# Turning a transpose into the place where candidate cells are folded: one product each on GpSimd, more matmuls on TensorE

## The chip, the cores and the metric

One core of a Trainium2 chip runs the whole program. The metric is the device time in microseconds of one execution, the median of several. Engines: PE is TensorE, DVE is VectorE, ACT is ScalarE, POOL is GpSimd, SP is SyncE, which issues the DMAs.

## What is computed

```python
frames = x.reshape(32, 313, 128)             # padded audio
h = einsum('bfh,kh->bfk', frames, D)         # DCT
h = h + attention(layernorm(h))              # within each of the 32 clips
# peer expert layer on layernorm(h), 8 heads:
s0, s1 = ...                                 # scores against 64 + 64 keys
sc0, ix0 = top_k(s0, 16); sc1, ix1 = top_k(s1, 16)
cs = sc0[..., :, None] + sc1[..., None, :]   # 16 x 16 sums per head
ci = ix0[..., :, None] + ix1[..., None, :]
fs, pos = top_k(cs, 16); fi = ci[pos]; w = softmax(fs)
inner = hidden . expert_down[fi]; act = gelu(inner)
h = h + sum((act * w) * expert_up[fi])
```

Of the 256 sums of a head only those at (i, j) with (i + 1)(j + 1) <= 16 can be among the 16 largest. The kernel forms 54 cells that hold these, in five rectangles (`CAND`, line 28). Since an index is a sum of two numbers below 64, only 128 expert rows are ever addressed.

## The kernel before

The 32 clips are taken in 16 pairs (`k`). A pair has 626 rows, in five tiles of 128 rows (`t` = 0 to 4), 80 tiles in all. The program of every engine is written out by hand in the same order (`drive`, line 266): for each tile four parts `p` = 0 to 3, in each of which `slot(k, t, p)` issues expert work and `front(k + 1, t, p)` the dense work of the next pair (DCT, attention, projection, statistics). Engines meet by semaphores. A tile's expert work is spread over five tiles' time, so that in one slot different engines work on different tiles.

What a tile goes through, with its lines:

- DVE takes the 16 largest of 64 scores for 16 half heads (p 1 and 2: `MAX8` L1016 and L1023, `MATCH_REPLACE8` L1019, `FIND_INDEX8` L1025 and L1028).
- POOL forms the sums of scores, `cs`, and of indices, `ci`, with one add per rectangle (`cells`, L822 to L830; `cs` in p 0, `ci` in p 1 after a wait for the `beta` of DVE).
- DVE takes the 16 largest of the 54 cells per head in p 3: `MAX8` over the first `NC8` = 44 cells (L1076), `MATCH_REPLACE8` (L1079), `MAX8` over 54 (L1082), `MATCH_REPLACE8` (L1085). The first 44 cells hold every cell that can be among the 8 largest. `c2` then has the value `PICKED` at the chosen cells.
- ACT makes the mask `m` from `c2` (L670) and the exponentials (L672). POOL multiplies by the reciprocal sum (`wz`, L869), then makes `Yw` = weights x mask and `Ye` = indices x mask (L873 to L877): one product over cells 0 to 31 and, for each, six small ones over the other 22 cells, which are put on 32 places of a second block (`share`, L833). Then it signals `y_full`. In p 3 it makes `bw` (L884, three products of 1024 elements), which waits for `w3_full` and `beta_full`.
- PE transposes and adds in p 3 (`rows`, L484, called at L532 to L536): for each half `a` of four heads it multiplies both blocks by the identity into the same 128 columns of PSUM, so that two cells which can't both be chosen share a row. `Ye` (bf16) goes to `STE`, `Yw` (f32) to `U`. A float32 matmul shows as two instructions in the trace.
- DVE reads `STE` in p 1 of the next tile: `hi` (L1035, L1040), `lo` (L1042), then eight comparisons of 1024 bf16 elements into `alpha` (L1049) and four into `beta` (L1055). This stretch is called the alpha phase below.
- ACT and PE split the weights in `U` into three bf16 parts (L677, L705, L708 on ACT, `less` L495 on PE), PE multiplies `alpha` and `bw` (L528, 16 matmuls in each part p, the first of a tile waits for `bw_full`).

Dense work that lies around it: at (2,1) DVE forms a seed (L953, L902), POOL runs 12 small Newton steps (L752), ACT makes `hid` (L639), PE transposes it at (2,2) (L394) and multiplies by `WcT` at (2,2) and (3,0) (L437). PE's statistics, called VAR below (L446, L447), come at (3,2). DVE reads them at (3,3) in `front`, behind its p 3 work (L978), and PE's `rows` for slot (2,3) lies in this chain. At (3,3) POOL starts another Newton chain when DVE has read VAR. `inner` (L459 to L470) has matmuls whose weights have 32 columns, with results at 32, 64 and 96 of the partitions.

Of the kernel before, what the change touches and what calls it, by code (L numbers as in the profile page):

```python
# [8 lines left out]
BF16 = mybir.dt.bfloat16  # L9
I32 = mybir.dt.int32  # L10
U32 = mybir.dt.uint32
ALU = mybir.AluOpType
# [14 lines left out]

CAND = [(0, 1, 16, 0), (1, 1, 8, 16), (2, 2, 5, 24), (4, 4, 3, 34), (8, 8, 1, 46)]
NC = 54
NC8 = 44  # L30
NX, NY = 32, 4
NS = 4
NG, NQ = 4, 32
# [44 lines left out]
def build(nc, x, Wq, bq, ln_g, ln_b, keys0, keys1, down, up, ident_d, dct_d, indc_d, sel_d, row8_d, sel3_d, out):  # L78
# [4 lines left out]
    with ctx:  # L83
# [93 lines left out]
        m = sb("m", [128, H, NC])  # L177
        wexp = sb("wexp", [128, H, NC])
        wz = sb("wz", [128, H, NC])
        Yw = sb("Yw", [128, 2, H, 32])  # L180
        Ye = sb("Ye", [128, 2, H, 32], BF16)
        wp = sb("wp", [128, 3, 3, 256], BF16)
        hi = sb("hi", [128, NS, 256], BF16)
        lo = sb("lo", [128, 256], BF16)
# [184 lines left out]
        def _(pe):  # L369
# [114 lines left out]
            def rows(src, eye, dst, end):  # L484

                for a in range(2):
                    for blk in range(2):
                        cells = src[:, blk, 4 * a:4 * a + 4, :].rearrange("p h r -> p (h r)")
                        last = mm(dst[:, 128 * a:128 * a + 128], cells, eye[:], start=(a == 0 and blk == 0),  # L489
                                  stop=(end and a == 1 and blk == 1), skip_group_check=True)  # L490
                return last

            def less(buf, i):
# [248 lines left out]
        def _(pool):  # L742
# [12 lines left out]
            def setup():  # L755
                nc.gpsimd.memset(xin[:], 0.0)
                nc.gpsimd.memset(ss[0][:], 1.0)
                nc.gpsimd.memset(ss[1][:], 1.0)
                nc.gpsimd.memset(c15[:], 1.5)
                nc.gpsimd.memset(one[:], 1.0)  # L760
                nc.gpsimd.memset(kp[:], 0.0).then_inc(s["zeroed"], 1)
                nc.gpsimd.memset(xns[:], 1.0)
                nc.gpsimd.memset(stdin[:], 0.0)
                nc.gpsimd.memset(Gd[:], 0.0)
                nc.gpsimd.memset(Yw[:], 0.0)
                nc.gpsimd.memset(Ye[:], 0.0)
                nc.gpsimd.memset(cneg64[:], -SHIFT)
                nc.gpsimd.memset(cpick[:], PICKED + 1.0)
                nc.gpsimd.memset(cquart[:], -0.75).then_inc(s["zeroed"], 1)
                pool.wait_ge(s["zeroed"], 2)  # L770
                nc.gpsimd.memset(stdin[:, :, 0, :, 8:9], 1.0)
                pool.wait_ge(s["kseed_full"], 1)
                newton(ky[:], kxh[:], ka[:], c15[0:64, 0:2], s["knewton"], 0)
# [48 lines left out]
            def cells(dst, v, done):  # L822

                halves = v.rearrange("p (h a) r -> p h a r", a=2)
                for i0, ni, nj, off in CAND:
                    o = dst[:, :, off:off + ni * nj].rearrange("p h (i j) -> p h i j", i=ni)
                    a0 = halves[:, :, 0, i0:i0 + ni].unsqueeze(3).to_broadcast([128, H, ni, nj])
                    a1 = halves[:, :, 1, 0:nj].unsqueeze(2).to_broadcast([128, H, ni, nj])
                    last = tt(o, a0, a1, ALU.add)  # L829
                last.then_inc(done, 1)  # L830


            share = [(slice(34, 44, 3), slice(12, 16)), (slice(35, 45, 3), slice(8, 12)),  # L833
                     (slice(46, 50), slice(20, 24)), (slice(50, 54), slice(4, 8)),
                     (slice(32, 33), slice(28, 29)), (slice(36, 37), slice(27, 28))]

            def slot(k, t, p):
                n = NT * k + t
# [26 lines left out]
                if p == 2 and exists(k, t, 2):  # L865
# [5 lines left out]
                    pool.wait_ge(s["m_full"], n - 1)  # L871
                    after(pool, s["st_full"], n - 2)
                    for Y, src in ((Yw, wz[:]), (Ye, ci[:, buf, :, :])):  # L873
                        tt(Y[:, 0, :, :], src[:, :, 0:32], m[:, :, 0:32], ALU.mult)
                        for cell, row in share:
                            last = tt(Y[:, 1, :, row], src[:, :, cell], m[:, :, cell], ALU.mult)
                    last.then_inc(s["y_full"], 1)  # L877
                if p == 3 and exists(k, t, 3):
                    buf = RING[(t - 3) % NT]
# [298 lines left out]
```

## Time and profile before

| | |
|---|---|
| median of 3 runs | 2131.66 us (2131.37 to 2132.61) |
| the profiled execution | 2132.51 us, its span 2130.3 us |
| mean granted PE clock | 0.729 of 2.4 GHz |
| DVE | busy 2008.6 us (94%), 16198 instructions |
| PE | 1682.7 us (79%) |
| POOL | 1578.8 us (74%) |
| ACT | 1108.1 us (52%) |
| DMA | 10 GB/s over the span |
| chain that ended last | DVE 68%, PE 14%, POOL 8%, issue 6%, ACT 3% |

The shares of the chain tell on which engine's work the end depended, step by step, and DVE's idle time tells where something else was late. A pair takes some 125 us, a tile some 25 us.

### The profile page before, as it was taken

The page shows a single profiled execution, that of the slowest core. Times are in us where ns is not written, and L with a number is a line of the kernel's source. Part 1 is how long each engine was busy: PE and PEld are TensorE (multiplying, and loading weights), DVE is VectorE, ACT ScalarE, POOL GpSimd, SP SyncE. Part 2 cuts the span into 40 slices and gives each one's busy share as a digit, 9 for nine tenths or more (in the row PEclk, how much of TensorE's full clock was granted, in tenths as well). Part 3 has the DMA queues.
Part 4 walks back from the last instruction along what each step waited for, and adds up shares of the span by engine and source line. Part 5 has one row for each costly group of instructions (what it writes and reads, how often), then busy time and mean ns, then how long its engine had stood idle before and what let it go on. Part 6 is the DMA issues. An engine that isn't in the chain of part 4 may idle for free.

```text
span 2130.3 us, 48144 instructions
## 1 busy us (share of the span) xinstructions
PE 1682.7 (79%) x10975; PEld 1311.4 (62%) x10975; DVE 2008.6 (94%) x16198; ACT 1108.1 (52%) x3515; POOL 1578.8 (74%) x3519
## 2 busy tenths in 40 slices
PE   5567698877869887797888779788877988887666
PEld 3336576655747665575766657666665756666455
DVE  3299999999999999999999999999999999999993
ACT  3344555565555556555555555545555564554443
POOL 2237788787778878777887877788787877878775
PEclk9676877677776777768677686867767686776655
DMA  1000000000000000000000000000000000000000
GB/s 34 13 9 2 18 7 13 14 6 18 6 18 6 8 18 8 18 6 19 7 6 18 9 18 6 18 6 6 19 9 16 9 18 6 6 12 9 6 8 9
DMA packets 46676, 24.86 MB, mean 12 GB/s; under 512 B 4955, under 2 KB 46116, under 8 KB 46390
## 3 DMA queue, kind: packets, MB, share of 16 engines
q1 hardware_dynamic: 46390, 21.80, 3.7%
q8 instruction: 88, 1.44, 0.3%
q14 instruction: 198, 1.62, 0.3%
HBM read 11.52 MB, written 10.26 MB: 10 GB/s over the span
## 4 chain that ended last, share of the span: by engine, by line
DVE 68%; PE 14%; POOL 8%; issue 6%; ACT 3%; another core or an unknown queue 0%; SPq 0%; DMA 0%; DVEq 0%; POOLq 0%; ACTq 0%
DVE hrest L1019 10%; DVE alpha L1049 8%; DVE idx L1025 8%; DVE idx L1028 8%; DVE vals L1016 6%; DVE vals L1023 5%; DVE crest L1079 4%; DVE c L1085 4%; PE FB L446 3%; PE FB L437 3%; PE QB L528 3%; DVE top L1082 2%; POOL bw L884 2%; DVE top L1076 2%; DVE beta L1055 2%
## 5 line engine op out<-in xcount | busy, mean ns | idle before, releaser
L528 PE MATMUL QB<-bw,alpha 128*128 128x48 bf16 x5120 | 553.3, 277 | 62.7 <-issue 62.0
L528 PEld LDWEIGHTS QB<-bw,alpha 128*128 128x128 bf16 x5120 | 521.5, 151 | 101.9 <-issue 93.0
L884 POOL TENSOR_TENSOR bw<-beta,wp 128x1024 bf16<-128x1024 bf16 x240 | 503.9, 2129 | 10.3 <-ACT wp L708 9.9
L722 ACT ACTIVATE WD<-QB 32x96 f32<-32x96 f32 x1280 | 307.2, 240 | 91.9 <-PE QB L528 80.4
L1049 DVE TENSOR_SCALAR alpha<-hi 128x1024 bf16<-128x1024 bf16 x640 | 270.0, 493 | 0.0
L480 PE MATMUL SC<-WK,hidT 128*128 128x512 f32 x320 | 225.3, 794 | 38.8 <-ACT hidT L655 23.9
L829 POOL TENSOR_TENSOR ci<-idxf 128x64 f32<-128x64 f32 (+3 forms) x400 | 123.9, 343 | 177.2 <-DVE beta L1055 176.9
L1025 DVE FIND_INDEX8 idx<-vals,sraw 128x8 uint32<-128x64 f32 x1280 | 250.5, 218 | 0.0
L1028 DVE FIND_INDEX8 idx<-vals,hrest 128x8 uint32<-128x64 f32 x1280 | 250.5, 219 | 0.0
L1019 DVE MATCH_REPLACE8 hrest<-vals,sraw 128x64 f32<-128x64 f32 x1280 | 250.2, 209 | 0.0
L1016 DVE MAX8 vals<-sraw 128x8 f32<-128x64 f32 x1280 | 169.2, 209 | 0.0
L1023 DVE MAX8 vals<-hrest 128x8 f32<-128x64 f32 x1280 | 167.3, 208 | 0.0
L752 POOL TENSOR_TENSOR sa<-sy 128x6 f32<-128x6 f32 x96 | 19.7, 205 | 193.0 <-DVE sy L902 188.0
L715 ACT ACTIVATE ofin<-QB 128x128 f32<-128x128 f32 x80 | 22.2, 277 | 263.9 <-PE QB L528 261.0
L829 POOL TENSOR_TENSOR cs<-vs 128x64 f32<-128x64 f32 (+3 forms) x400 | 137.0, 375 | 6.3
L437 PE MATMUL FB<-hidTn,WcT 128*128 128x313 f32 x256 | 121.3, 633 | 19.9 <-ACT hidTn L645 10.8
L480 PEld LDWEIGHTS SC<-WK,hidT 128*128 128x128 f32 x320 | 72.4, 246 | 97.7 <-issue 53.4
L446 PE MATMUL FB<-indc,sq 128*128 128x24 f32 x640 | 127.4, 347 | 0.7 <-ACT sq L650 0.7
L516 PE MATMUL QB<-upR,Gd 128*128 128x128 f32 x640 | 123.7, 355 | 4.5 <-issue 4.2
L702 ACT ACTIVATE sraw<-SC 128x1024 f32<-128x1024 f32 x80 | 83.1, 1038 | 83.1 <-PE SC L481 82.4
L446 PEld LDWEIGHTS FB<-indc,sq 128*128 128x128 f32 x640 | 122.9, 285 | 1.1 <-ACT sq L650 1.1
L489 PE MATMUL U<-ident,Yw 128*128 128x128 f32 x640 | 121.1, 350 | 0.0
(206 smaller groups left out, 4079.9 us busy)
## 6 DMA issues: line engine op xcount, KB each, us to landing
res<-h_scratch SPq DMA_DIRECT2D x80, 64.0 KB, 1.8
xin<-in_x SPq DMA_DIRECT2D x32, 128.0 KB
h_scratch<-h2n SPq DMA_DIRECT2D x32, 128.0 KB
out<-ofin SPq DMA_DIRECT2D x64, 64.0 KB, 1.6
h_scratch<-h2n SPq DMA_DIRECT2D x32, 28.5 KB
out<-ofin SPq DMA_DIRECT2D x16, 57.0 KB
xin<-in_x SPq DMA_DIRECT2D x32, 28.0 KB
xin<-in_x SPq DMA_DIRECT2D x32, 0.2 KB
```

The source lines that it names most:

```text
L446: mm(bank[:, 40 * tt:40 * tt + 24], sq[:, c, cols], indc[:, c, :], start=(c == 0), stop=(c == 3))
L480: mm(SC[:, cols], hidT[:, START[t1]:START[t1] + 128], WK[:, cols], start=True, stop=False)
L528: last = mm(bank[:, 48 * u:48 * u + 48], alpha[:, buf, a, :, 8 * p + u], bwv[:, :, a, :, 8 * p + u], start=(a == 0), stop=(a == 1))
L722: last = A(WD[r, RING[(t - 4) % NT], :, 8 * p:8 * p + 8], blocks[r, :, :, g], ACT.Copy)
L829: last = tt(o, a0, a1, ALU.add)
L884: last = tt(bw[:, buf, NY * i:NY * i + NY, :], beta[:, buf, :, :], wp[:, buf, i, :].unsqueeze(1).to_broadcast([128, NY, 256]), ALU.mult)
L1016: V.max(vals[:, buf, i, 0:8], raw[i]).then_inc(chain, 1)
L1019: V.match_replace(rest[i], vals[:, buf, i, 0:8], raw[i], -1e30).then_inc(chain, 1)
L1023: V.max(vals[:, buf, i, 8:16], rest[i]).then_inc(chain, 1)
L1025: V.max_index(idx[:, buf, i, 0:8], vals[:, buf, i, 0:8], raw[i]).then_inc(chain, 1)
L1028: last = V.max_index(idx[:, buf, i, 8:16], vals[:, buf, i, 8:16], rest[i])
L1049: last = V.tensor_scalar(a8[:, :, :, xx, :], h8, float(NY * xx), None, ALU.is_equal)
```

## The change

`Yw` and `Ye` are stored cell by cell ([54 cells, 8 heads] in each partition), so POOL makes each with one product over all 54 cells and 8 heads, writing with a step of 8 elements. The sharing of rows moves to PE: `rows` multiplies cells 0 to 15 and 16 to 31 as before (a = 0, 1), and then six more groups of 16 or 32 columns each (`FOLD`), written on top of partitions 32, 64 or 96 of the same PSUM columns. Rectangle (4,4,3), cells 34 to 45, is stored with i innermost, so that each fold is a run of cells and the first 38 cells hold all that can be among the 8 largest: `NC8` goes from 44 to 38. Two memsets of the setup go.

```diff
-NC8 = 44
+NC8 = 38
+FOLD = [(slice(34, 38), 0, 12), (slice(38, 42), 0, 8), (slice(42, 46), 0, 4), (slice(50, 54), 0, 4),
+        (slice(46, 50), 1, 4), (slice(32, 34), 1, 12)]
...
-        Yw = sb("Yw", [128, 2, H, 32])
-        Ye = sb("Ye", [128, 2, H, 32], BF16)
+        Yw = sb("Yw", [128, NC, H])
+        Ye = sb("Ye", [128, NC, H], BF16)
...
                 for a in range(2):
-                    for blk in range(2):
-                        cells = src[:, blk, 4 * a:4 * a + 4, :].rearrange("p h r -> p (h r)")
-                        last = mm(dst[:, 128 * a:128 * a + 128], cells, eye[:], start=(a == 0 and blk == 0),
-                                  stop=(end and a == 1 and blk == 1), skip_group_check=True)
+                    last = mm(dst[:, 128 * a:128 * a + 128], src[:, 16 * a:16 * a + 16, :].rearrange("p c h -> p (c h)"),
+                              eye[:], start=(a == 0), stop=False, skip_group_check=True)
+                for i, (cells, a, row) in enumerate(FOLD):
+                    w = H * (cells.stop - cells.start)
+                    last = mm(dst[8 * row:8 * row + w, 128 * a:128 * a + 128],
+                              src[:, cells, :].rearrange("p c h -> p (c h)"), eye[:], start=False,
+                              stop=(end and i == len(FOLD) - 1), skip_group_check=True)
...
-                nc.gpsimd.memset(Yw[:], 0.0)
-                nc.gpsimd.memset(Ye[:], 0.0)
...
-                    o = dst[:, :, off:off + ni * nj].rearrange("p h (i j) -> p h i j", i=ni)
+                    by = "p h (j i) -> p h i j" if i0 == 4 else "p h (i j) -> p h i j"
+                    o = dst[:, :, off:off + ni * nj].rearrange(by, i=ni)
...
-            share = [(slice(34, 44, 3), slice(12, 16)), (slice(35, 45, 3), slice(8, 12)),
-                     (slice(46, 50), slice(20, 24)), (slice(50, 54), slice(4, 8)),
-                     (slice(32, 33), slice(28, 29)), (slice(36, 37), slice(27, 28))]
...
                     for Y, src in ((Yw, wz[:]), (Ye, ci[:, buf, :, :])):
-                        tt(Y[:, 0, :, :], src[:, :, 0:32], m[:, :, 0:32], ALU.mult)
-                        for cell, row in share:
-                            last = tt(Y[:, 1, :, row], src[:, :, cell], m[:, :, cell], ALU.mult)
+                        last = tt(Y[:].rearrange("p c h -> p h c"), src, m[:], ALU.mult)
```

## Rows read from the trace of the kernel before

**Rows 1.** The page: busy time, share of the span and instructions of each engine
```profile
PE 1682.7 (79%) x10975; PEld 1311.4 (62%) x10975; DVE 2008.6 (94%) x16198; ACT 1108.1 (52%) x3515; POOL 1578.8 (74%) x3519
```

**Rows 2.** Waits of DVE: line, releaser, us in total, times, longest
```profile
DVE v L978 <- PE FB L447: 27.7, 10, 22.7
```

**Rows 3.** Timeline, two pairs' ends of VAR: start us, us, engine, line, [idle before]
```profile
1046.35 0.20 DVE L978 TENSOR_SCALAR v<-FB 128x40 f32<-128x40 f32 x1 [0.49 <-PE FB L447]
...
1168.56 0.59 PE L447 MATMUL FB<-WB,hidTn 128*128 128x16 f32 x2
...
1170.98 0.20 DVE L978 TENSOR_SCALAR v<-FB 128x40 f32<-128x40 f32 x1
```

**Rows 4.** Groups by line and form, DVE's MAX8: count, busy us, mean ns
```profile
L1082 DVE MAX8 top<-crest 128x8 f32<-128x54 f32 x640 | 81.4, 200 | 0.0
...
L1076 DVE MAX8 top<-cs 128x8 f32<-128x44 f32 x640 | 74.8, 190 | 0.0
```

**Rows 5.** Timeline of POOL, from the first product of one tile
```profile
1015.14 0.73 POOL L874 TENSOR_TENSOR Yw<-wz,m 128x256 f32<-128x256 f32 x1
...
1017.78 1.33 POOL L876 TENSOR_TENSOR Ye<-ci,m 128x32 bf16<-128x32 f32 x6
1019.04 6.32 POOL L884 TENSOR_TENSOR bw<-beta,wp 128x1024 bf16<-128x1024 bf16 x3
...
1027.54 1.55 POOL L829 TENSOR_TENSOR cs<-vs 128x128 f32<-128x128 f32 x5
```

**Rows 6.** Groups by line and form, POOL's longer products
```profile
L884 POOL TENSOR_TENSOR bw<-beta,wp 128x1024 bf16<-128x1024 bf16 x240 | 503.9, 2129 | 10.3 <-ACT wp L708 9.9
...
L869 POOL TENSOR_TENSOR wz<-wexp,rz 128x432 f32<-128x432 f32 x80 | 72.7, 909 | 3.7 <-DVE rz L1067 3.7
```

**Rows 7.** Groups at 1016.1 us, and at 1016.6 us, of POOL
```profile
L876 POOL TENSOR_TENSOR Yw<-wz,m 128x32 f32<-128x32 f32 x2 | 0.5, 286 | 0.0
...
L876 POOL TENSOR_TENSOR Yw<-wz,m 128x32 f32<-128x32 f32 x1 | 0.3, 265 | 0.0
```

**Rows 8.** Busy us (instructions) in four alpha phases: PE, PEld, DVE, ACT, POOL, PEclk
```profile
1027.54:1032.50 4.96, 4.96 (x13) 2.55 (x12) 4.92 (x19) 3.78 (x11) 1.54 (x5) 0.74 0.00 2
1052.12:1059.08 6.96, 4.58 (x88) 4.20 (x87) 6.92 (x19) 6.10 (x16) 6.33 (x15) 0.75 0.03 8
1077.61:1082.11 4.50, 1.98 (x18) 1.64 (x17) 4.47 (x19) 4.38 (x14) 0.00 (x0) 0.91 0.02 5
1102.16:1108.77 6.61, 6.61 (x26) 3.24 (x25) 6.58 (x19) 4.97 (x14) 5.63 (x13) 0.77 0.01 2
```

**Rows 9.** Timeline of PE around `rows` in the chain to VAR
```profile
1022.99 0.40 PE L489 MATMUL EB<-identb,Ye 128*128 128x128 bf16 x4
1023.23 1.11 PE L489 MATMUL U<-ident,Yw 128*128 128x128 f32 x8
1025.46 1.74 PE L528 MATMUL QB<-bw,alpha 128*128 128x48 bf16 x16 [1.11 <-issue]
```

**Rows 10.** Timeline of PE: `rows`, then the start and the end of `inner`
```profile
1172.82 0.61 PE L489 MATMUL EB<-identb,Ye 128*128 128x128 bf16 x4
...
1175.17 0.68 PE L467 MATMUL SC<-hidT,DT 128*32 128x128 f32 x8
...
1177.33 0.89 PE L528 MATMUL QB<-bw,alpha 128*128 128x48 bf16 x7
```

**Rows 11.** Busy us in these two calls of `rows`, columns as in rows 8
```profile
1022.99:1024.34 1.35, 1.35 (x15) 1.16 (x12) 1.35 (x12) 1.10 (x5) 1.35 (x2) 1.00 0.00 0
1172.82:1175.17 2.35, 2.35 (x14) 2.13 (x13) 2.35 (x24) 2.08 (x8) 1.80 (x7) 0.50 0.18 52
```

**Rows 12.** Timeline of POOL and DVE in the last tiles
```profile
2076.88 6.27 POOL L884 TENSOR_TENSOR bw<-beta,wp 128x1024 bf16<-128x1024 bf16 x3
...
2077.97 6.23 DVE L1040 TENSOR_SCALAR hi<-hi 128x256 bf16<-128x256 bf16 x3
...
2093.31 6.26 POOL L884 TENSOR_TENSOR bw<-beta,wp 128x1024 bf16<-128x1024 bf16 x3
```

## The prediction

> **What bounds the kernel now.** I read the page's busy times first: DVE is busy 94% of the span, PE 79%, POOL 74% [rows 1]. Then the waits of DVE, to see where it isn't the bound. In the middle of the run it waits in one place only, for VAR: 10 times, 27.7 us, of which the first, in the fill, is 22.7, so nine waits of 0.55 us on average, 5.0 us together [rows 2]. The timeline at this place shows two kinds of pairs. In nine pairs DVE comes 0.4 to 0.7 us too early (at 1046 us it idles 0.49); in five others it comes 1.9 us after VAR was done (VAR's last matmul ends at 1169.15, DVE's L978 follows its own work at 1170.98), and in an early one 5.8 us after [rows 3]. So two chains of nearly equal length run from DVE's seed at (2,1) to L978 at (3,3): DVE's own work, and POOL's Newton steps, `hid`, PE's projection, `rows`, the quads and VAR. Everywhere else DVE alone sets the pace. What makes DVE faster counts in full outside this stretch, and inside it only as far as PE's chain gets faster too.
>
> Last I asked whether DVE's work always takes as long. The table of alpha phases says no: the same 19 instructions take 4.50 us while POOL is idle, 4.96 with 1.54 us of POOL's work inside, 6.61 with 5.63 and 6.96 with 6.33 [rows 8]. Each us of POOL's work in an alpha phase costs DVE 0.30 us (0.46 / 1.54) to 0.39 (2.46 / 6.33). POOL is thus on the path, though it is idle a quarter of the time. Where it comes before, its adds must end before DVE's alpha phase starts.
>
> **The change part by part.**
>
> (a) **MAX8 over 38 cells in place of 44.** 54 cells take 200 ns, 44 take 190, 1 ns per cell [rows 4]. 6 cells x 1.0 ns x 640 = 3.8 us of DVE.
>
> (b) **POOL's products.** Now `Yw` starts at 1015.14 and `bw` at 1019.04: 3.90 us for 14 instructions [rows 5]. After, there are two of 432 elements. A product that reads two full tensors takes 0.73 us for 256 elements [rows 5], and 2.129 us for 1024 [rows 6]: 1.82 ns per element, so 0.73 + 176 x 0.00182 = 1.05 us for 432. `wz` with its 432 took 0.909, but one operand is repeated [rows 6]. That is the lower end. The write has a step of 8 elements, which no POOL instruction of the trace has. The nearest row is a read with a step of 3: 286 ns against 265 for 32 elements [rows 7], 0.6 ns per element for two stepped reads. I take the same for the one stepped write: 1.05 + 432 x 0.0006 = 1.3 us. Two take 2.6, and POOL is s = 1.3 us earlier with `bw`. Bounds: s = 1.8 with no penalty; s = 0 if a product takes 1.95 us, nearly twice the unstepped one. Below nothing is possible, since nothing in the trace excludes a penalty over twofold.
>
> GPSIMD Engine Reference of the Trainium skill, section Performance pitfalls for Q7 kernels, says that reads whose step is over 8 bytes cost half as much again. The trace shows 8% for a step of 12 bytes [rows 7]; the page says nothing of writes. Applied to these writes it is a rival below.
>
> (c) **What s does to alpha phases.** Two of five tiles gain. At (3,1) (14 pairs show it) `cs` starts at 1027.54 and lasts 1.55, inside the alpha phase [rows 5, 8]; 1.3 us earlier nearly all of it lies before the phase: 0.46 x 14 = 6.4 us. At (1,1) POOL goes without a pause from its products through `bw`, a Newton chain and its adds into the phase; 1.3 us less overlap at (6.61 - 4.50) / 5.63 = 0.37 is 0.48, x 15 = 7.2 us. At (4,1) the POOL chain is started by DVE's L978, so it isn't earlier: nothing. The other two have no overlap: nothing.
>
> (d) **PE's folds and the chain to VAR.** `rows` now takes 1.35 us at a granted clock of 1.00 (2.4 GHz) and 2.35 at 0.50 (1.2 GHz), for four products of each kind [rows 11]. After, there are two full ones and six narrow ones of each kind. `inner` shows what narrow ones cost: 16 float32 products of 128 columns and 16 of 32, to all four column groups, take from 1175.17 to 1177.33, 2.16 us [rows 10], at 0.50. One after the other they would take about 10 us (2.0 us for four full ones [rows 10, 11], so 0.5 and 0.125 each). So four groups run side by side. The six folds go to groups 3, 2, 1, 1, 1, 3: three places in a row, with the two full ones five in place of four. I take + 1.35 / 4 = 0.34 us; the upper end, nothing side by side, is + 1.35. In the chain to VAR PE now stands still for 1.11 us behind `rows` [rows 9], until POOL's `bw` ends at 1025.36 [rows 5]. After, `rows` ends at 1024.34 + 0.34 = 1024.68, and `bw` at 1025.36 - 1.3 = 1024.06. PE goes on 0.78 us earlier than at 1025.46.
>
> DVE's own part of the stretch gets 0.46 (c) + 0.10 (MAX8 of two tiles) = 0.56 us shorter. Where DVE waits now, the pair gains what PE gains, 0.78, which is 0.22 more than (a) and (c) count: x 9 = 2.0 us. In the pairs with 1.9 us of slack nothing is added. In the other tiles the folds lie on PE's idle time: DVE needs only the `Ye` part of `rows`, first in order, and waits for it nowhere in the middle.
>
> TensorEngine Tiling (Array Packing) of the Trainium skill, section Tiling Modes, says that a change of tiling mode drains TensorE, and the change brings four per tile. The trace shows none between `rows` and `inner`: `inner` starts at 1175.17, when `rows` ends [rows 10, 11]. The page gives no price, so the sum stays.
>
> (e) **The last tiles.** There the `bw` of POOL (2076.88 to 2083.15) holds up a DVE instruction that else takes 0.2 us (L1040, three in 6.23 us), and PE's quads too [rows 12]. Two sets of products lie on this path, ahead of the `bw` at 2076.88 and at 2093.31 [rows 12]: 2 x 1.3 = 2.6, and some 0.4 of overlap goes in the alpha phase before: 3.0 us. The two memsets of the setup lie beside loads: nothing. The turned rectangle changes the step of one write of `cs` and `ci` each; at 96 elements x 0.6 ns it is 0.06 us ahead of `bw`, nothing to count.
>
> Sum: 3.8 + 6.4 + 7.2 + 2.0 + 3.0 = 22.4 us. The profiled execution took 2132.51, its span 2130.3; the median of the runs is 0.85 below the profiled one, and I take the gain from the median: 2131.7 - 22.4 = 2109.3 us, in a profile about 2110.
>
> **The rivals.**
>
> *All waits for VAR go.* PE's clock is 0.50 or 1.00 by stretches [rows 11], and a PE that no longer stands still may keep 1.00 in the projection behind. With s at 1.8 too: 3.8 + 6.4 + 15 x 0.67 + 5.0 + 4.0 = 29.2, so 2102.5. For it: the slack pairs have exactly this. Against: VAR itself runs at 0.50 for most of its time in both kinds.
>
> *Folds don't overlap.* Then `rows` ends at 1025.69 and PE is 0.23 later than now, and what DVE gains in the stretch is lost too: -9 x (0.23 + 0.56) = -7.1 in place of +2.0. 22.4 - 9.1 = 13.3: 2118.4. Against it stands `inner`; for it, that three folds in a row go to one group, and that the others are few.
>
> *Stepped writes cost half as much again* (the rule on reads named above, taken for writes). 1.58 us per product, s = 0.74: (a) 3.8; (c) 0.22 x 14 + 0.27 x 15 = 7.1; (d) PE still gains 0.78 against 0.32 of DVE, 9 x 0.46 = 4.1; (e) 1.7. Sum 16.7: 2115.0.
>
> *Stepped writes cost double, POOL isn't earlier.* s = 0: 3.8 from MAX8, less 0.9 that DVE now waits for VAR: 2.9, so 2128.8. The change then has nothing but its shorter MAX8.
>
> *Slower: PE's chain becomes the bound.* If the folds run one by one and narrow columns leave the clock at 0.50 at (2,3) in every pair, `rows` takes 4.7 us there and ends at 1027.69, 2.23 us later than PE goes on now. Nine pairs lose 9 x 2.23 = 20.1, the five with slack 0.9 each, together 24.6; what is gained outside the stretch, 2.3 + 7.2 + 3.0 = 12.5, stays. 2131.7 + 12 = 2144. It decides from about 1.4 us per waiting pair (12.5 / 9). For it: the clock is low in these very matmuls in other places [rows 11]. Against: at (2,3) they stand at 1.00 after a long busy stretch.
>
> **How the numbers follow.** Forecast 0.42, all waits gone 0.13, folds in a row 0.15, half as much again 0.12, double 0.10, slower 0.08. The predicted time is that of the forecast, 2109. About 0.2% (4.3 us) can be told from no change: faster 0.82, same 0.10, slower 0.08. The range leaves out the last two, 0.18, and reaches from 2101 (s = 1.8 and all waits gone, with 1.5 us for what the clock may add) to 2126 (folds in a row together with half as much again, some 2123, and a few us for the clock).
>
> **What would show it.** MAX8 of L1076 at 184 ns. Two POOL products of 1.3 us each and `bw` 1.3 us after where it would be without; 1.05 or 1.95 tell the ends. The alpha phase at (3,1) at 4.5 us and at (1,1) at 6.1; at (4,1) as before. Behind `rows` at (2,3) no gap of PE; `rows` itself 1.7 us at clock 1.00 (forecast) or 2.7 (in a row). The wait of DVE for VAR, 0.55 us in nine pairs, at 0.3. The prediction is wrong if POOL's products aren't shorter, if alpha phases don't follow POOL's overlap, or if waits for VAR grow in pairs that had none.

## The result and the profile after

The changed kernel takes 2116.74 us (2116.2 to 2117.8, 4 runs) against 2132.14 of the kernel before in the same runs: a ratio of 0.9926, 95% interval 0.9909 to 0.9944, so 15.4 us faster, 12 to 19. The forecast was 22.4 us, 2109.3; the measured time lies inside its range of 2101 to 2126. Its profiled execution took 2116.96 us with a span of 2115.2 and a mean granted clock of 0.744.

Busy times on the page of the changed kernel (as rows 1):

```profile
PE 1727.9 (82%) x11935; PEld 1335.8 (63%) x11935; DVE 1993.5 (94%) x16198; ACT 1108.9 (52%) x3515; POOL 1501.2 (71%) x2557
```

DVE has 15.1 us less work with the same 16198 instructions, and the span is 15.1 us shorter. Since MAX8 explains 3.9 us of this (below), the larger part is DVE's time for instructions that the diff doesn't touch. PE has 45 us more work, POOL 78 us less.

The groups by line and form, changed kernel, with POOL's products and MAX8 (as rows 4 and 6): count, busy us, mean ns.

```profile
L874 POOL TENSOR_TENSOR Ye<-ci,m 128x432 bf16<-128x432 f32 x80 | 173.3, 2167 | 0.0
...
L874 POOL TENSOR_TENSOR Yw<-wz,m 128x432 f32<-128x432 f32 x80 | 89.0, 1113 | 6.3
...
L1074 DVE MAX8 top<-cs 128x8 f32<-128x38 f32 x640 | 70.9, 185 | 0.0
```

The two products differ in the type that they write (and in which tensor they read beside the mask), and the record of the bf16 one is twice as long. The timeline of POOL in the same tile as rows 5, changed kernel:

```profile
1007.13 1.10 POOL L874 TENSOR_TENSOR Yw<-wz,m 128x432 f32<-128x432 f32 x1
1008.19 2.12 POOL L874 TENSOR_TENSOR Ye<-ci,m 128x432 bf16<-128x432 f32 x1
1009.91 6.38 POOL L882 TENSOR_TENSOR bw<-beta,wp 128x1024 bf16<-128x1024 bf16 x3
1017.66 0.46 POOL L842 TENSOR_TENSOR ws<-WD 128x128 f32<-128x128 f32 x1 [1.38 <-ACT WD L727]
```

From the first product to `bw` it is 2.78 us in place of 3.90 [rows 5]: POOL is 1.12 us earlier. From start to start the float32 product holds POOL up for 1.06 us and the bf16 one for 1.72, since `bw` starts before `Ye` is recorded as ended. But then POOL stands still for 1.38 us ahead of `ws`, for ACT's `WD`: part of what was won is lost here.

The timeline of PE at the same place (as rows 9), changed kernel:

```profile
1016.21 0.29 PE L489 MATMUL EB<-identb,Ye 128*128 128x128 bf16 x2
1016.43 0.35 PE L493 MATMUL EB<-identb,Ye 128*32 128x128 bf16 x6
1016.71 0.71 PE L489 MATMUL U<-ident,Yw 128*128 128x128 f32 x4
1017.35 0.86 PE L493 MATMUL U<-ident,Yw 128*32 128x128 f32 x12
1018.14 1.77 PE L533 MATMUL QB<-bw,alpha 128*128 128x48 bf16 x16
```

`rows` takes 1.93 us until the next matmul starts (1016.21 to 1018.14). To the end of its last record it is 2.00, against the 1.35 of before [rows 9, 11], which is taken that way. The gap of PE behind it is gone. Six float32 folds take 0.79 us, two and a half times a full product (0.64 / 2 = 0.32). The six bf16 folds take 0.28, and a full bf16 product 0.11.

The waits of DVE and of POOL in the changed kernel (as rows 2): in total us, times, longest.

```profile
DVE v L976 <- PE FB L449: 28.6, 7, 22.0
...
POOL ci L833 <- DVE beta L1053: 136.1, 40, 11.7
POOL ci L833 <- ACT idxf L694: 59.0, 11, 5.9
...
POOL ws L842 <- ACT WD L727: 17.6, 8, 9.1
```

Without the first one, DVE waits 6.6 us for VAR in six pairs (1.1 each), before 5.0 in nine. POOL waits 59 us for ACT's `idxf`, where it waited 0.3 before. Most of that is time in which it would have waited for `beta` in any case: both waits together are 195 us, before 177. POOL's wait for ACT's `wp` ahead of `bw` grows too, from 9.9 us to 36.2, but not in the tiles that lead to the alpha phases at (3,1) and (1,1). The pairs now alternate: a quick one (123.9 us) in which VAR comes 1.2 to 1.4 us before it is needed, and a slow one (125.3 us) in which it comes 1.1 us late. Before they took 124.7, 125.5 and 125.3 us in turn.

The stages of a slow pair's chain to VAR (from PE's transposes of `hid` through the projection; `rows` to the quads; VAR) in the changed kernel, columns as in rows 8; the first and the last of these stages in a quick pair; and four alpha phases: (3,1) of a slow and a quick pair, (1,1) of a pair behind a slow one and of one behind a quick one.

```profile
1005.85:1016.21 10.36, 9.59 (x40) 6.97 (x41) 10.36 (x105) 4.81 (x14) 10.28 (x8) 0.59 0.01 2
1016.20:1028.20 12.00, 11.44 (x91) 8.68 (x89) 11.93 (x83) 9.99 (x29) 7.39 (x17) 0.99 0.05 13
1028.20:1038.85 10.65, 10.65 (x54) 10.65 (x51) 9.69 (x100) 0.97 (x4) 8.09 (x5) 0.50 0.00 0
...
1131.52:1140.54 9.02, 8.24 (x41) 5.86 (x42) 9.02 (x94) 4.81 (x14) 8.94 (x8) 0.68 0.01 3
1152.53:1161.65 9.12, 9.12 (x53) 9.12 (x52) 9.12 (x95) 0.97 (x4) 8.85 (x5) 0.60 0.00 1
...
1019.41:1024.53 5.12, 4.56 (x19) 2.57 (x18) 5.09 (x19) 4.35 (x13) 2.21 (x6) 1.00 0.01 2
1145.09:1149.65 4.56, 4.00 (x16) 2.18 (x16) 4.53 (x19) 3.54 (x10) 0.64 (x3) 1.00 0.01 2
1094.30:1101.26 6.96, 5.84 (x32) 3.42 (x31) 6.93 (x19) 5.58 (x16) 6.30 (x14) 1.00 0.00 0
1218.57:1224.85 6.28, 5.62 (x20) 2.73 (x21) 6.25 (x19) 3.52 (x9) 4.80 (x11) 0.73 0.01 1
```

The alpha phase follows POOL's share as before [rows 8], but only every other pair has the relief: at (3,1) 4.56 us with 0.64 us of POOL, or 5.12 with 2.21; at (1,1) 6.28 with 4.80, or 6.96 with 6.30. (The 19 instructions of such a row are the 17 of the phase and two that touch its ends.) In a slow pair VAR runs at 0.50 (1.2 GHz) from beginning to end, in a quick one at 0.60 on average.

What makes POOL late for the alpha phase at (1,1) begins at (4,3). First `rows` there in the kernel before, at 2.4 GHz, then in the changed kernel behind a slow pair's VAR, with what PE, ACT and POOL do next:

```profile
1192.35 0.40 PE L489 MATMUL EB<-identb,Ye 128*128 128x128 bf16 x4
1193.53 1.15 PE L394 MATMUL FB<-ident,xin 128*128 128x128 f32 x6
```

```profile
1064.39 0.39 PE L489 MATMUL EB<-identb,Ye 128*128 128x128 bf16 x2
...
1066.30 1.50 PE L493 MATMUL U<-ident,Yw 128*32 128x128 f32 x12
1067.73 1.50 PE L396 MATMUL FB<-ident,xin 128*128 128x128 f32 x5
...
1068.75 0.43 ACT L603 ACTIVATE xT<-FB 128x313 f32<-128x313 f32 x1 [2.98 <-PE FB L396]
...
1075.77 0.50 ACT L694 ACTIVATE idxf<-idx,cquart 128x256 f32<-128x256 uint32 x1
...
1076.42 1.55 POOL L833 TENSOR_TENSOR ci<-idxf 128x128 f32<-128x128 f32 x5 [5.85 <-ACT idxf L694]
```

Before, `rows` at (4,3) kept PE for 1.2 us at 2.4 GHz or 2.2 at 1.2 GHz. Now it runs at 1.2 GHz in most pairs, quick and slow, and takes 3.3 us. Where it does so behind a quick pair's VAR, it starts 7.1 us before DVE's alpha phase at (0,1), and `idxf` starts 4.4 us into that phase, whose `beta` ends at 4.5: POOL's `ci` is 0.5 us late. Behind a slow pair's VAR PE is 1.2 us later, `idxf` starts 5.5 us into the phase, and `ci` is 1.6 us late.

### The profile page after: what moved, and what is told of

It is laid out like the page before. It is cut to its first block, busy times and chain, and to the rows that moved or that the text cites. A ratio compares the mean times of both kernels' runs of the same rounds, so it can differ in the third digit from the quotient of the medians.

```text
span 2115.2 us, 49102 instructions
## 1 busy us (share of the span) xinstructions
PE 1727.9 (82%) x11935; PEld 1335.8 (63%) x11935; DVE 1993.5 (94%) x16198; ACT 1108.9 (52%) x3515; POOL 1501.2 (71%) x2557
## 4 chain that ended last, share of the span: by engine, by line
DVE 78%; PE 12%; issue 4%; ACT 2%; POOL 2%; another core or an unknown queue 0%; SPq 0%; DMA 0%; DVEq 0%; POOLq 0%; ACTq 0%
DVE hrest L1017 11%; DVE idx L1023 10%; DVE idx L1026 10%; DVE alpha L1047 9%; DVE vals L1014 7%; DVE vals L1021 6%; DVE crest L1077 5%; DVE c L1083 5%; DVE top L1080 3%; PE FB L448 3%; DVE top L1074 2%; DVE beta L1053 2%; PE QB L533 2%; PE FB L439 2%; DVE hi L1038 2%
## 5 line engine op out<-in xcount | busy, mean ns | idle before, releaser
L882 POOL TENSOR_TENSOR bw<-beta,wp 128x1024 bf16<-128x1024 bf16 x240 | 508.1, 2146 | 36.5 <-ACT wp L713 36.2
L1047 DVE TENSOR_SCALAR alpha<-hi 128x1024 bf16<-128x1024 bf16 x640 | 265.6, 488 | 0.0
L482 PE MATMUL SC<-WK,hidT 128*128 128x512 f32 x320 | 211.0, 747 | 35.4 <-ACT hidT L660 33.4
L874 POOL TENSOR_TENSOR Ye<-ci,m 128x432 bf16<-128x432 f32 x80 | 173.3, 2167 | 0.0
L521 PE MATMUL QB<-upR,Gd 128*128 128x128 f32 x640 | 136.3, 382 | 4.5 <-issue 4.2
L448 PE MATMUL FB<-indc,sq 128*128 128x24 f32 x640 | 134.3, 359 | 0.7 <-ACT sq L655 0.7
L448 PEld LDWEIGHTS FB<-indc,sq 128*128 128x128 f32 x640 | 129.8, 299 | 1.1 <-ACT sq L655 1.1
L521 PEld LDWEIGHTS QB<-upR,Gd 128*128 128x128 f32 x640 | 124.6, 286 | 8.4 <-issue 6.8
L500 PE MATMUL U<-wp,minusb 128*128 128x256 bf16 x160 | 52.7, 329 | 92.6 <-ACT wp L710 81.3
L439 PE MATMUL FB<-hidTn,WcT 128*128 128x313 f32 x256 | 109.3, 577 | 20.0 <-ACT hidTn L650 10.9
## 6 DMA issues: line engine op xcount, KB each, us to landing
h_scratch<-h2n SPq DMA_DIRECT2D x32, 28.5 KB
```

The lines of the kernel that those rows point to most:

```text
L448: mm(bank[:, 40 * tt:40 * tt + 24], sq[:, c, cols], indc[:, c, :], start=(c == 0), stop=(c == 3))
L521: mm(FO, Gd[:, y, :], upR[:, y, :], start=(y == 0), stop=False)
L882: last = tt(bw[:, buf, NY * i:NY * i + NY, :], beta[:, buf, :, :], wp[:, buf, i, :].unsqueeze(1).to_broadcast([128, NY, 256]), ALU.mult)
L1047: last = V.tensor_scalar(a8[:, :, :, xx, :], h8, float(NY * xx), None, ALU.is_equal)
```

## The experiments

All times are medians; "before" is the kernel before in the same runs, 2130.6 to 2132.3 us, and ratios are to it. The changed kernel was timed only for the result above (ratio 0.9926). Since "before" itself lies up to 1.8 us apart, a difference to 2116.74 of 2 us or less isn't shown by the times alone. A profile is of one execution, up to 3.4 us from the median. The sums over alpha phases below are over the first 15 pairs, as the excess over 4.50 us each: in the kernel before 7.1 us at (3,1) and 30.2 at (1,1), in the changed one 4.5 and 28.5.

**MAX8 alone.**

```diff
-NC8 = 44
+NC8 = 38
...
+                    by = "p h (j i) -> p h i j" if i0 == 4 else "p h (i j) -> p h i j"
...
-            share = [(slice(34, 44, 3), slice(12, 16)), (slice(35, 45, 3), slice(8, 12)),
+            share = [(slice(34, 38), slice(12, 16)), (slice(38, 42), slice(8, 12)),
...
-                     (slice(32, 33), slice(28, 29)), (slice(36, 37), slice(27, 28))]
+                     (slice(32, 33), slice(28, 29)), (slice(42, 43), slice(27, 28))]
```

> The kernel before with nothing changed but the turned rectangle and MAX8 over 38 cells (the products of POOL and the transposes of PE stay). If time goes by DVE's work and the waits for VAR: 3.9 us less work of DVE, of which 0.1 us per waiting pair is lost in longer waits, so about 3 us faster (2129). If instead the clock of PE follows each small shift of the program, the pattern of pairs changes and the time may move by several us either way (2124 to 2136).

2129.32 us, ratio 0.9986 (0.9977 to 0.9996): 2.8 us faster, 0.9 to 4.9. DVE's MAX8 has 3.9 us less, and its waits for VAR rise from 27.7 to 30.5 us in the profile (of an execution of 2131.4 us). The pattern of pairs did change, too: 13 pairs wait in place of nine. So this part of the change is worth about 3 us, as expected here; the interval holds the 3.8 of the prediction as well. What it frees is partly taken back at VAR.

**POOL as late as before.**

```diff
-                    for Y, src in ((Yw, wz[:]), (Ye, ci[:, buf, :, :])):
+                    for Y, src in ((Yx, wz[:]), (Yw, wz[:]), (Ye, ci[:, buf, :, :])):
```

`Yx` is a new tile of the shape and type of `Yw`.

> The changed kernel with one more product on POOL (the weights a second time, into a tile that nobody reads), so that POOL is as late with bw as before the change, and folds and MAX8 stay. If POOL's earlier bw brought what isn't MAX8, this gives it back: some 2.2 us in the last tiles and 4 to 6 us in the alpha phases, 2123 to 2126, with alpha phases at (3,1) and (1,1) as long as before. If POOL isn't what counts, it stays within 2 us of the changed kernel (2117).

2128.48 us (2125.06 to 2129.26), ratio 0.9982 (0.9973 to 0.9992). One product of 1.1 us that nobody reads, as long as the lead that the changed kernel has won, costs 11.7 of the 15.4 us. (1,1) has an excess of 32.5 us, more than before the change, and (3,1) 6.2. The median is above the range that I expected, in the direction of the first theory. The profile is of a faster execution (2126.49). In it 9.5 us are lost: 4.3 between the first VAR and the last, 3.3 in the last tiles, and 1.9 before the first VAR, a start that varies between kernels (below). The first two, 7.6 us, are what the profiles put down to POOL's lead. So POOL's lead ahead of `bw` carries at least half of the gain, and by the medians nearly all that isn't MAX8, though POOL is idle 29% of the time.

**No folds.** The cells 32 to 53 are left out of the result.

```diff
-                for i, (cells, a, row) in enumerate(FOLD):
+                for i, (cells, a, row) in enumerate([]):
```

The second full product of `Yw` then closes the sum in PSUM (`stop`), as the last fold did.

> The changed kernel without the six folds in either transpose: cells 32 to 53 are left out of the result. rows then takes 0.9 us at 2.4 GHz and 1.5 at 1.2, against 1.9 and 3.3. If the folds' time on PE took the missing part of the gain (later VAR, and in pairs at 1.2 GHz a later ACT and so a later POOL), the waits for VAR fall from 6.6 us to under 2 and the alpha phase at (1,1) is 6.2 us in all pairs: 2107 to 2110. If the missing part lies with POOL's slow product of indices, it stays at 2115 to 2117.

2111.53 us (2110.02 to 2112.8), ratio 0.9905 (0.9889 to 0.9922): the folds cost 5.2 us. The waits in this kernel:

```profile
POOL ci L833 <- DVE beta L1053: 210.5, 50, 11.8
DVE v L976 <- PE FB L449: 24.3, 5, 21.5
...
POOL ci L833 <- ACT idxf L694: 0.3, 1, 0.3
```

POOL no longer waits for `idxf`, and (1,1) has an excess of 23.4 us with the relief in every pair. The waits for VAR are 2.8 us, and there is still a slow pair in three. The time misses the expected 2107 to 2110 by 1.5 us and the waits for VAR the expected 2 by 0.8; the places were those expected. `idxf` now starts at most 2.4 us into the alpha phase at (0,1), well ahead of `beta`. So the chain is PE's `rows` at (4,3), then the dense work behind it, then ACT, in whose queue `idxf` stands behind that work, then POOL. The edit takes the folds out of all five tiles, so that it is (4,3) rests on the times above and on the next experiment.

**`idxf` ahead of the dense work.** PE is untouched.

```diff
-                if p == 0 and exists(k, t, 1):
-                    buf = RING[(t - 1) % NT]
-                    act.wait_ge(s["halves_full"], n)
-                    after(act, s["ci_full"], n - 1)
-                    A(idxf[:], idx[:, buf, :, :], ACT.Identity, bias=cquart[:]).then_inc(s["idxf_full"], 1)
...
+                if p == 3 and exists(k, t, 0):
+                    act.wait_ge(s["halves_full"], n + 1)
+                    after(act, s["ci_full"], n)
+                    A(idxf[:], idx[:, RING[t], :, :], ACT.Identity, bias=cquart[:]).then_inc(s["idxf_full"], 1)
```

> The changed kernel with ACT's conversion of the indices moved from p 0 of the next tile to the end of p 3, ahead of the dense work of the front. Nothing changes on PE. If the alpha phases at (1,1) stay long in the slow pairs because POOL waits for ACT's idxf (59 us in the changed kernel), these waits go, that phase is 6.2 us in every pair, and the time is 3 to 5 us less (2112 to 2114), with VAR chains and their waits as in the changed kernel. If POOL was late for another reason, the time stays at 2116 to 2117, or rises where ACT now waits for DVE's halves.

2115.20 us (2115.01 to 2115.51), ratio 0.9927 (0.991 to 0.9943). That is 1.5 us under the changed kernel's 2116.74, but "before" is 1.6 us lower here too, and the ratios are the same: the times show no gain, where I had expected 3 to 5 us. The profiles show one of 2.4 us between the first VAR and the last. The mechanism is right: no wait of POOL for `idxf` any more, the excess at (1,1) falls from 28.5 to 24.0 us, 6.1 to 6.3 us in every pair. Little of it reached the time, and DVE's rows tell why. The longest of DVE's norms at (0,1), first the changed kernel, then this one:

```profile
L991 DVE SCALAR_TENSOR_TENSOR n<-v,n 128x80 f32<-128x80 f32 x16 | 4.7, 296 | 0.5
```

```profile
L990 DVE SCALAR_TENSOR_TENSOR n<-v,n 128x80 f32<-128x80 f32 x16 | 6.4, 398 | 0.5
```

POOL's `ci`, no longer late, now runs right behind `beta`, beside these steps of DVE: from the end of the alpha phase to the next candidate stage it takes 10.1 us, where it took 9.7 in the pairs in which POOL was late. Of 0.7 us won at (1,1) 0.4 is given back at (0,1). Over 15 pairs the norms give back 2.8 us of 4.5.

**The product of indices with a packed write**, alone and with the early `idxf`:

```diff
-                        last = tt(Y[:].rearrange("p c h -> p h c"), src, m[:], ALU.mult)
+                        if Y is Ye:
+                            last = tt(Y[:], src.rearrange("p h c -> p c h"), m[:].rearrange("p h c -> p c h"), ALU.mult)
+                        else:
+                            last = tt(Y[:].rearrange("p c h -> p h c"), src, m[:], ALU.mult)
```

> The changed kernel with the product of indices taken cell by cell: its two reads have a step of 54 elements (216 bytes) and its write in bf16 is packed. If only the stepped bf16 write is dear (2.12 us against 1.06 for the float32 one), the product takes 1.1 to 1.6 us and the kernel gains 1 to 4 us (2113 to 2116). If stepped reads are as dear, it takes 2 us or more and nothing is gained (2117 or later).

2116.47 us (2116.34 to 2116.83), ratio 0.9928 (0.9912 to 0.9945). The product takes 1751 ns in place of 2167, but `bw` starts 1.62 us behind its start where it was 1.72, and nothing clear is gained: by what POOL's queue pays, the stepped reads cost about what the stepped write did.

> The same move together with the product of indices taken cell by cell (packed bf16 write, stepped reads). If POOL's work ahead of bw counts by itself, this adds 0.5 to 1.5 us to the gain of the move alone (2111 to 2113). If not, it equals it.

2113.35 us (2113.04 to 2115.34), ratio 0.992 (0.9904 to 0.9937), 1.9 us below the early `idxf` alone in the same runs (one of its four times lies inside the other's range), with an excess of 22.9 us at (1,1). The excess at (1,1) explains 1.1 us of it.

**Another order of the folds.**

```diff
-FOLD = [(slice(34, 38), 0, 12), (slice(38, 42), 0, 8), (slice(42, 46), 0, 4), (slice(50, 54), 0, 4),
-        (slice(46, 50), 1, 4), (slice(32, 34), 1, 12)]
+FOLD = [(slice(42, 46), 0, 4), (slice(34, 38), 0, 12), (slice(38, 42), 0, 8), (slice(50, 54), 0, 4),
+        (slice(32, 34), 1, 12), (slice(46, 50), 1, 4)]
```

> The changed kernel with the six folds in another order, by column group 1, 3, 2, 1, 3, 1 in place of 3, 2, 1, 1, 1, 3, so that no more than one follows another in the same group. If same-group folds wait for each other, the six float32 folds take about 0.7 us in place of 0.79 at 2.4 GHz, the pairs keep their pattern and the time is within 2 us of the changed kernel. If the price is that of issuing 18 instructions, the folds take the same time, and so does the kernel (2116 to 2118).

2119.05 us (2117.95 to 2120.07). The float32 folds take 0.77 us in place of 0.79, `rows` 1.91: the order is worth nothing. The time is 2.3 us above the changed kernel, and outside what I expected. That is not from the pairs, whose pattern is the same: DVE reads the first VAR at 75.5 us in this profile and at 73.2 in that of the changed kernel, and in the other kernels shown here between 72.8 and 75.1. What sets this start was not tried.

**`cs` ahead of `ws`.** POOL's five adds for `cs` come before the three that need ACT's `WD`.

```diff
-                if p == 0 and exists(k, t, 5):
-                    pool.wait_ge(s["wd_full"], 4 * (n - 4))
...
                     cells(cs[:, buf, :, :], vs[:], s["cs_full"])
+                if p == 0 and exists(k, t, 5):
+                    pool.wait_ge(s["wd_full"], 4 * (n - 4))
```

> The changed kernel with POOL's sums of scores (vs, cs) ahead of its adds of PE's results (ws, G) in p 0. If the alpha phase at (3,1) kept its length because POOL stands behind ACT's WD (1.4 us at 1016 us) with cs behind it, cs now lies before that phase: its excess falls from 4.5 us to under 2. The time falls only by what isn't taken back at VAR: in the slow pairs DVE waits longer for it, so 0 to 3 us (2114 to 2117). If POOL was late for another reason, the excess stays at 4 or more.

2114.76 us (2111.36 to 2115.36), ratio 0.9917 (0.9901 to 0.9934). Its alpha phases at (3,1) and (1,1), columns as in rows 8:

```profile
1017.04:1021.53 4.49, 3.94 (x17) 2.40 (x16) 4.46 (x19) 3.72 (x12) 0.50 (x2) 1.00 0.00 2
1091.84:1098.53 6.69, 5.57 (x29) 3.14 (x29) 6.66 (x19) 2.98 (x10) 6.01 (x14) 1.00 0.00 0
```

At (3,1) the excess is 0.0 us in all 15 pairs, from 4.5. So what stood ahead of `cs` in POOL's queue kept it late. The edit takes `cs` past the wait for `WD` and past three adds of 1.5 us as well. That the wait was the cause is worked out from the profile of the changed kernel: the six pairs without relief are those in which POOL waited 1.3 to 1.4 us for `WD`. Without it `cs`, which starts at 1019.87 in the pair shown, would end some 0.6 us inside the phase, as it does in the quick pairs. In the four slow pairs that are left the wait for VAR grows from 1.1 to 1.8 us, so that nothing is gained in them; two pairs that were slow are now quick. This profile is of the fastest execution, 3.4 us under the median, and the median doesn't differ clearly from the changed kernel's.

**POOL's writes by themselves.** Two programs with POOL alone, 432 elements per product, 8 of each; most of the result is left out.

The first program writes float32 at steps of 4, 8 and 32 bytes (f1, f2, f8) and bf16 at 2, 4, 8 and 16 bytes (h1, h2, h4, h8), and has two forms with packed writes whose reads are both at a step of 216 bytes (fr, hr). The second writes only bf16: packed (plain), at 4, 8 and 16 bytes with the values between them written by the same instruction (twomix, fourmix, eightmix), and at 16 and 32 bytes with each value alone (eight, sixteen).

> Nothing of the computation: POOL alone makes products of 432 elements, 8 times each, into tiles with different steps and types (the result is left out but for 128 rows of ones). If a step of over 8 bytes in a write costs half as much again whatever the type, f8 (float32, step 32 bytes), h8 (bf16, 16 bytes) and h4 take 1.6 us against 1.06 for f1 and h1. If the trouble is that a stepped bf16 write touches part of a word, h2, h4 and h8 all take 2.1 us, and f2 and f8 1.06. Stepped reads of 216 bytes (fr, hr) take 1.6 to 1.75.

Groups of single products in the first program (f1; h4; h8), and the two with stepped reads:

```profile
L60 POOL TENSOR_TENSOR f<-a,b 128x432 f32<-128x432 f32 x1 | 1.1, 1093 | 0.1
...
L60 POOL TENSOR_TENSOR h<-a,b 128x432 bf16<-128x432 f32 x1 | 1.2, 1157 | 0.0
...
L60 POOL TENSOR_TENSOR h<-a,b 128x432 bf16<-128x432 f32 x1 | 2.1, 2111 | 0.0
...
L60 POOL TENSOR_TENSOR fr<-a,b 128x432 f32<-128x432 f32 x8 | 13.1, 1641 | 0.0
L60 POOL TENSOR_TENSOR hr<-a,b 128x432 bf16<-128x432 f32 x8 | 13.0, 1630 | 0.0
```

All three float32 forms take 1.09 to 1.10 us, bf16 at 2, 4 and 8 bytes 1.09, 1.10 and 1.16, and only bf16 at 16 bytes 2.11. Neither theory said this. From its start to the start of the next product, which is what the queue pays, the last one takes 1.71 us and the other six forms 1.05.

> POOL alone again, 432 elements each, all written in bf16: packed; eight values interleaved at a step of 16 bytes (as in the change); the same step with each value alone in its 16 bytes; alone in 32 bytes; four interleaved at 8 bytes; two at 4 bytes. The result is left out but for 128 rows of ones. If the step of 16 bytes is what costs, the first lone one takes 2.1 us and that of 32 bytes as much or more, and those of 8 and 4 bytes 1.1. If interleaving is what costs (a value next to one written shortly before), the lone ones take 1.1 us and all interleaved ones 2.1.

```profile
L57 POOL TENSOR_TENSOR eight<-a,b 128x432 bf16<-128x432 f32 x8 | 18.5, 2313 | 0.0
L57 POOL TENSOR_TENSOR sixteen<-a,b 128x432 bf16<-128x432 f32 x8 | 17.7, 2212 | 0.0
L57 POOL TENSOR_TENSOR eightmix<-a,b 128x432 bf16<-128x432 f32 x8 | 16.9, 2107 | 0.0
L57 POOL TENSOR_TENSOR fourmix<-a,b 128x432 bf16<-128x432 f32 x8 | 10.7, 1335 | 0.0
L57 POOL TENSOR_TENSOR twomix<-a,b 128x432 bf16<-128x432 f32 x8 | 8.9, 1109 | 0.0
L57 POOL TENSOR_TENSOR plain<-a,b 128x432 bf16<-128x432 f32 x8 | 8.7, 1092 | 0.6
```

A value alone in its 16 or 32 bytes is as slow as an interleaved one (from start to start 1.91 and 1.84 us, against 1.71), so for bf16 it is the step and not the interleaving. Why float32 at 32 bytes is free stays open. GPSIMD Engine Reference of the Trainium skill (Performance pitfalls for Q7 kernels) has half as much again for reads over 8 bytes. The reads at 216 bytes agree (1.64 against 1.09 us). The writes, of which the page says nothing, don't follow that rule: float32 pays nothing, and bf16 at 16 bytes pays more.

**Everything stored cell by cell from the start**, on top of the early `idxf`:

```diff
-        ci = sb("ci", [128, 3, H, NC])
+        ci = sb("ci", [128, 3, NC, H])
...
-                    A(m[:], c2[:], ACT.Relu, scale=-1.0, bias=cpick[:]).then_inc(s["m_full"], 1)
+                    A(m[:].rearrange("p c h -> p h c"), c2[:], ACT.Relu, scale=-1.0, bias=cpick[:]).then_inc(s["m_full"], 1)
...
-                        last = tt(Y[:].rearrange("p c h -> p h c"), src, m[:], ALU.mult)
+                        last = tt(Y[:], src, m[:], ALU.mult)
```

and likewise for the exponentials and `wz`.

> The kernel with the early idxf, with indices, mask and weights stored cell by cell from the start: ci, mask and exponentials are written with steps (float32, by POOL and ACT), and both products read and write packed. If only the write of bf16 with a step of 16 bytes is dear, both products take 1.05 us, bw starts 1.8 us earlier than before the change, and the time is 1.5 to 3 us under the early idxf alone (2112 to 2113.7). If ACT's stepped writes cost, its mask and exponentials take over 0.65 and 0.55 us and the gain goes.

2102.63 us (2101.36 to 2103.61), ratio 0.9857 (0.9841 to 0.9874): 29.7 us faster than before, 14.1 us faster than the changed kernel, and far more than I expected. Its products, ACT's mask and its wait for VAR:

```profile
L873 POOL TENSOR_TENSOR Yw<-wz,m 128x432 f32<-128x432 f32 x80 | 89.6, 1120 | 6.3
L675 ACT ACTIVATE m<-c,cpick 128x432 f32<-128x432 f32 x80 | 88.9, 1112 | 0.0
L873 POOL TENSOR_TENSOR Ye<-ci,m 128x432 bf16<-128x432 f32 x80 | 88.5, 1106 | 0.0
```

```profile
DVE v L975 <- PE FB L449: 21.9, 1, 21.9
```

Both products take 1.1 us. ACT's stepped writes cost what the expectation warned of (the mask 1.11 us, before 0.65), and the gain is there all the same: ACT is busy 56%. `wz` takes 1.11 us in place of 0.90. The excess at (1,1) falls to 18.7 us. The rest is at VAR: no pair waits, all chains from `hid` to VAR take 31.2 to 31.3 us, where the changed kernel had 30.1 or 33.1, and every pair takes 123.2 to 123.8 us. Of the 14.1 us, 9.8 are the excess at (1,1), and the waits for VAR another 6.6; the changed kernel is better by 0.6 at (3,1), 0.5 at (4,1) and 2.9 in the norms. Why PE's clock gives 31.3 us in every pair here wasn't separated from POOL's lead, so how much of the gain is the order of the data and how much the pattern of the clock stays open.

**Four folds in place of six**, on top of that: the first rectangle stored backwards, cells 34 to 45 folded by one matmul of 96 columns.

```diff
+FOLD = [(slice(34, 46), 0, 0), (slice(50, 54), 0, 8), (slice(46, 50), 1, 4), (slice(32, 34), 1, 12)]
...
+                    if i0 == 0:
+                        o = o[:, :, :, ::-1]
```

> The same, with the first rectangle stored backwards, so that the 12 cells 34 to 45 lie on partitions 0 to 95 and are folded by one matmul of 96 columns: four folds in place of six. If the price of folds is that of issuing small matmuls, rows takes 0.15 to 0.3 us less at 2.4 GHz and the time falls by 1 to 3 us (2109 to 2112). If 96 columns cost more than three side by side, it stays or rises.

2102.42 us (2100.31 to 2104.24), ratio 0.9859 (0.9843 to 0.9875), no difference to the six. `rows` took 1.64 us at the same place, against 1.93, as expected: fewer matmuls take less time, and one of 96 columns costs no more than three side by side. But no pair waits for VAR any more, and PE's time is worth nothing.

## Why the prediction was right, and where it was off

The time lies in the range and the direction and the main mechanism hold: DVE sets the pace, and its alpha phases grow with POOL's work inside. Term by term:

- (a) MAX8: 3.8 us forecast, 3.9 less busy time and 2.8 us of time measured alone.
- (b) POOL's products: 1.3 us each forecast. From start to start the float32 one takes 1.06, without any penalty, the bf16 one 1.72, some 60% more (their records are 1.11 and 2.17 long). The nearest row, a stepped read, said nothing of either: the two errors nearly cancel, 2.78 us in place of 2.6, and s is 1.12 us in place of 1.3. This is a right number by luck.
- (c) at (3,1): 6.4 us forecast, 2.6 measured. The step that failed is "1.3 us earlier nearly all of it lies before the phase". I moved POOL's whole queue by s, but its next instruction behind `bw`, `ws`, waits for `WD` in the slow pairs. Moving `cs` ahead of `ws` took the excess to zero.
- (c) at (1,1): 7.2 us forecast, 1.7 measured. The relief per phase is right where it comes (6.1 to 6.4 us, forecast 6.1), but it comes only in every other pair. The step that failed is in (d), "in the other tiles the folds lie on PE's idle time". I looked at DVE's waits alone. At (4,3) `rows` takes 3.3 us at 1.2 GHz in place of 1.2 or 2.2 (the 2.35 of rows 10 and 11 is at (3,3)), and behind it wait the dense work, ACT with `idxf` in its queue, and POOL's `ci`. In a slow pair PE comes to it 1.2 us later, and both together make POOL late. Both the kernel without folds and that with an early `idxf` bring the relief back in all pairs. The late `ci` has a good side that I didn't foresee either: it no longer runs beside DVE's norms at (0,1), which take 2.7 us less over 15 pairs.
- (d) `rows` in the chain: 1.7 us forecast at 2.4 GHz, 2.00 measured in the same way. The float32 part grows from 1.11 us to 1.50 (forecast 1.39, five places in place of four), its six folds taking two and a half places. The bf16 part doubles, from 0.24 us to 0.50 (forecast 0.30): I priced a bf16 fold by its share of a full product, while the six take 47 ns each. PE did go on earlier, without the gap: 1.93 us behind the start of `rows`, before 2.47, so 0.54 us where 0.78 was forecast. The forecast that waits for VAR shrink from 5.0 to 3 us was wrong, they grew to 6.6, since the chain now takes 33.1 us in six pairs (before 32.4 to 32.8 in nine) and 30.1 in the rest. Two of the six are pairs that had no wait before, which the prediction names as a sign of being wrong: for VAR it was.
- (e) the last tiles: 3.0 us forecast; from the last VAR to the end it took 208.5 us, now 204.7, so 3.7.
- Not forecast: the first VAR comes 1.7 us earlier. It varies by that much between kernels that don't differ there.

Together: 22.4 forecast, less 3.8 at (3,1), less 5.5 at (1,1), less 3.6 at VAR, plus 0.7 and 1.7 at the ends, makes 11.9 of the 15.4. Of the remaining 3.5 us, 2.7 are DVE's norms at (0,1), and 0.8 I can't place; (4,1), forecast at nothing, has not moved (an excess of 36.4 us, now 36.3).

Of the rivals, the one of folds in a row (2118.4) has the nearest time, and for the wrong reason: folds do run side by side. The one of half as much again for stepped writes (2115.0) also gives nearly the time, and is wrong for both types: 1.06 and 1.72 us, where it has 1.58 for each. A time between rivals doesn't tell which of them holds, the rows do.

## What to carry to other kernels

Work on an engine that is idle more than a quarter of the time can still cost time, if its instructions slow the busiest engine while they overlap: here 1.1 us of POOL per tile, 88 us in all, moved the time by 11.7, about an eighth. Part of this came in the last tiles, where POOL lies on the path itself. When a queue is moved earlier, ask of each instruction behind it what it waits for; the first one that waits for another engine ends the gain. And when work is added to an engine with idle time, follow the queue behind it to the engine that comes after the next, not only to the one that sets the pace.

Try to store the data in the order that the last reader wants where it is first written, by the engine that has time for a stepped write: here that went with the largest gain of all, though the clock's pattern changed with it.

## What the runs showed of the hardware that I had not expected

- POOL writes 432 float32 elements at steps of 4, 8 and 32 bytes in 1.09 to 1.10 us, and bf16 at 2 and 4 bytes in 1.09 to 1.11; at 16 or 32 bytes bf16 takes 2.1 to 2.3 us, at 8 bytes 1.16 or 1.34. The record of such a slow one ends 0.4 us after the next one starts (2.12 us long, `bw` 1.72 behind), so the queue pays 1.7 to 1.9 us, where a packed write costs it 1.05.
- Two stepped reads at 216 bytes take 1.64 us in place of 1.09, 1.3 ns more per element. At 12 bytes they cost 8% [rows 7], but of an instruction of 32 elements, most of whose time doesn't grow with them: that is 0.6 to 0.8 ns per element.
- ACT's 432 float32 elements at a step of 32 bytes take 1.11 us in place of 0.65, so ACT pays for the step that POOL doesn't.
- Six float32 products with 16 to 32 weight columns, to three column groups, take 0.79 us, where full ones take 0.32 each: they overlap. In bf16 such a product takes about 47 ns. There was no gap at the change between full and narrow ones, 4 times per tile.
- Within one kernel PE's chain to VAR, the same instructions each time, takes 30.1 or 33.1 us (before the change 30.1 or 32.4 to 32.8). The difference goes with the granted clock: 9.0 us at 0.68 against 10.4 at 0.59 in the projection, 9.1 at 0.60 against 10.7 at 0.50 in VAR. The pattern over pairs changed with nearly every edit, and what sets it stays open.
